# A two-layer graph kernel: eight of 26 adjacency chunks taken as products instead of six, sums in nine pairs, and the copy of a finished head on VectorE

## The reference

```python
q = (x @ Wq.T).reshape(d, n, h)      # k, v alike; d = 128, n = 3327, h = 8
a = jnp.einsum('dnh,dmh->dnm', q, k) * scale
a = a + spatial_encoding + edge_encoding          # both are adj
a = jax.nn.softmax(a, axis=2)
out = jnp.einsum('dnm,dmh->dnh', a, v)
```

## Time and profile before

| | us |
|---|---|
| median of 3 runs | 11010.36 |
| range of the runs | 11007.11 to 11011.85 |
| the profiled execution, its own time | 11014.46 |
| its span in the profile | 11012.8 |

### The profile page before, as it was taken

One profiled execution on the slowest core, in us unless ns is written; L12 is line 12 of the kernel. 1 busy time (PEld: TensorE's weight loads), 2 busy tenths in 40 slices (PEclk: granted clock), 3 DMA queues, 4 the chain that ended last, 5 costly groups with the idle time before them and its releaser, 6 DMA issues. The chain is left out here.

```text
span 11012.8 us, 545250 instructions
## 1 busy us (share of the span) xinstructions
PE 10687.6 (97%) x216535; PEld 6688.6 (61%) x216535; DVE 10342.3 (94%) x10893; ACT 10389.9 (94%) x9224; POOL 6451.1 (59%) x3236
## 2 busy tenths in 40 slices
PE   8749999999999999999999999999999999999998
PEld 6616666666666666666666666666665666666666
DVE  7679999999999999999999999999999999999997
ACT  3359999999999999999999999999999999999996
POOL 4345666666665666666665666666665666666664
PEclk9889999999999999999999999999999999999999
DMA  6581111111112111111112111111112111111113
GB/s 220 171 263 55 41 41 41 41 42 42 41 42 79 41 41 41 41 41 41 42 42 81 41 41 41 41 41 41 41 41 81 41 41 41 41 41 41 41 41 83
DMA packets 572794, 649.12 MB, mean 59 GB/s; under 512 B 172173, under 2 KB 511251, under 8 KB 566867
## 3 DMA queue, kind: packets, MB, share of 16 engines
q1 hardware_dynamic: 570130, 617.66, 20.1%
q0 software_dynamic: 832, 1.71, 0.0%
HBM read 485.17 MB, written 133.77 MB: 56 GB/s over the span
## 5 line engine op out<-in xcount | busy, mean ns | idle before, releaser
L1075 DVE SCALAR_TENSOR_TENSOR at_double<-attention_adj_t,at_score 128x832 f32<-128x832 f32 x10240 | 9672.9, 1014 | 411.0 <-PE at_score L1019 396.2
L999 POOL TENSOR_TENSOR at_single<-at_single,attention_adj_t 128x832 f32<-128x832 f32 x3072 | 6114.8, 1991 | 3977.4 <-ACT at_single L1089 3944.0
L1092 ACT ACTIVATE at_double<-at_double 128x1664 f32<-128x1664 f32 x5120 | 8138.8, 1653 | 28.1 <-DVE at_double L1075 20.8
L1019 PE MATMUL at_score<-at_q,at_k 128*32 128x512 bf16 (+1 forms) x106496 | 7275.9, 350 | 72.5 <-DMA at_v<-v_scratch 46.3
L1035 PE MATMUL at_acc<-at_double,at_v 128*9 128x208 f32 x81920 | 5387.0, 339 | 0.7 <-ACT at_double L1092 0.6
L1019 PEld LDWEIGHTS at_score<-at_q,at_k 128*32 128x32 bf16 x106496 | 3529.9, 145 | 2586.1 <-DVE at_double L1075 1145.3
L1089 ACT ACTIVATE at_single<-at_score 128x832 f32<-128x832 f32 x3072 | 2828.4, 921 | 34.2 <-PE at_score L1019 34.2
L1035 PEld LDWEIGHTS at_acc<-at_double,at_v 128*9 128x9 f32 x81920 | 2080.6, 91 | 1002.3 <-issue 3.8
L1035 PE MATMUL at_acc<-at_single,at_v 128*9 128x208 f32 x24576 | 1615.4, 339 | 2.9 <-issue 2.8
L1035 PEld LDWEIGHTS at_acc<-at_single,at_v 128*9 128x9 f32 x24576 | 622.8, 91 | 307.3 <-issue 4.8
L287 POOL TENSOR_TENSOR layer_col_acc<-layer_col_acc,st_a_rows 128x3328 f32<-128x3328 f32 x26 | 189.2, 7277 | 181.3 <-DMA st_a_rows<-in_adj_dram 181.3
(11 more groups left out here) (123 smaller groups left out, 1288.1 us busy)
## 6 DMA issues: line engine op xcount, KB each, us to landing
at_k<-k_parts_scratch SPq DMA_DIRECT2D x1536, 156.0 KB
at_q<-q_parts_scratch SPq DMA_DIRECT2D x4608, 13.0 KB
at_v<-v_scratch SPq DMA_DIRECT2D x512, 112.5 KB
adj_t_scratch<-st_a_t SPq DMA_DIRECT2D x26, 1664.0 KB, 7.6
st_a_rows<-in_adj_dram SPq DMA_DIRECT2D x25, 1663.5 KB, 8.7
attention_adj_t<-adj_t_scratch SPq DMA_DIRECT2D x16, 2080.0 KB, 16.7
attended_scratch<-at_o SPq DMA_DIRECT2D x1920, 7.3 KB
q_parts_scratch<-pr_partsq SPq DMA_DIRECT2D x39, 512.0 KB, 4.6
```

Source lines behind the costliest of these rows:

```text
L999: pool.tensor_tensor(slot(n), slot(n), at[:, plan.chunk[n], :], ALU.mult).then_inc(multiplied, 1)
L1019: last = pe.matmul(score[plan.buffer(n)][32 * t:32 * (t + 1), a:b], keys[:, 32 * t:32 * (t + 1)], q[k][:, a:b], start=True, stop=True, til ...
L1075: dve.scalar_tensor_tensor(out=slot(n), in0=at[:, plan.chunk[n], :], scalar=2.0, in1=score[plan.buffer(n)][:, 0:NB], op0=ALU.mult, op1=ALU ...
L1092: act.activation(doubles[buffer][:], doubles[buffer][:], ACT.Exp).then_inc(exped, 1)
```

## The change

PRODUCTS goes from 6 to 8: eight chunks of the 26 are taken as products, 18 as sums in nine pairs. DOUBLES goes from 8 to 6 and SINGLES from 4 to 8 (20 buffers of 128 x 832 in both). `Steps` then gives each head the order `ssPssPssPssPssPssPssPssPss`, and ScalarE's order is P, pair, P, pair; two pairs follow each other without a P between only at a head's end (steps 21-22 and 24-25; then the P of the next head's step 2, then its pair 0-1). `stream_adjacency` stores eight chunks as exp(2a); its chunks 18 and 19 need an activation of 128 x 256 of their own. The groups at a change of block become sums 0-4 and 5-9, products 18-22 (steps 2 to 14), sums 10-14 (steps 15 to 21), products 23-25 (steps 17, 20, 23) and sums 15-17 (steps 22, 24, 25).

The copy of a finished head moves from ScalarE (KEEP_LAG) to VectorE, behind step 12 of the next head (KEEP_AFTER). The counts of `kept` and `stored` are shifted by one, since the first copy copies an empty `acc`. ScalarE's loop is then a plain loop over all 128 bodies. SCORE_LEAD goes from 8 to 9. The number of instructions in TensorE's loop body is as before.

```diff
--- before.py
+++ after.py
@@ -46,11 +46,11 @@
 COLT = 4
 QW = NB // COLT
 assert QW * COLT == NB
-DOUBLES = 8
-SINGLES = 4
+DOUBLES = 6
+SINGLES = 8
 GROUP = 4
 CHUNKS_AT_ONCE = 5
-PRODUCTS = 6
+PRODUCTS = 8
 LIMIT = 30.0
 
 
@@ -912,8 +912,8 @@
         LOADS = 16 * (PARTS + PARTS * PARTS + 1 + 3)
         STORES = 16 * COLT
         CLEARED = 8
-        SCORE_LEAD = 8
-        KEEP_LAG = 5
+        SCORE_LEAD = 9
+        KEEP_AFTER = 12
         assert GROUP * products % SINGLES == 0 and GROUP % 2 == 0
 
         first_of_group = {steps[0]: g for g, steps in enumerate(plan.groups)}
@@ -956,7 +956,7 @@
 
             with runs(sp):
                 for k in range(2):
-                    sp.sem_inc(stored[k], STORES)
+                    sp.sem_inc(stored[k], 2 * STORES)
                 sp.wait_ge(prefetched, 16 * len(Steps(PRODUCTS).prefetched))
                 if products:
                     for g in plan.prefetched:
@@ -981,7 +981,7 @@
                                 load_adjacency(b + 1, range(len(plan.groups)))
                         store(b, HEADS - 2 + k, k)
                 for k in range(2):
-                    sp.wait_ge(stored[k], STORES * (BLOCKS * HEADS // 2 + 1))
+                    sp.wait_ge(stored[k], STORES * (BLOCKS * HEADS // 2 + 2))
 
         @block.gpsimd
         def _(pool):
@@ -1064,6 +1064,14 @@
                 dve.wait_ge(k_zero, 2)
                 for k in range(2):
                     dve.memset(k_all[k][SHIFT_ROW:SHIFT_ROW + PARTS, 0:N], 1.0).then_inc(cleared, 1)
+
+                def keep_head(i, b, head):
+                    k = head % 2
+                    dve.wait_ge(used, STEPS * i + (b * BODIES * STEPS + (head + 1) * C + AHEAD))
+                    dve.wait_ge(stored[k], STORES * (GROUP // 2) * i + STORES * (b * BODIES * (GROUP // 2) + head // 2 + 2))
+                    dve.tensor_copy(o[k][:], acc[k][:, 0:QW]).then_inc(kept, 1)
+
+                dve.sem_inc(kept, 1)
                 for b in range(BLOCKS):
                     with dve.Fori(0, BODIES) as i:
                         for n in range(STEPS):
@@ -1074,6 +1082,9 @@
                                 dve.wait_ge(used, plan.used_by(i, plan.last_like(plan.slot, n)) + (b * BODIES * STEPS + AHEAD))
                                 dve.scalar_tensor_tensor(out=slot(n), in0=at[:, plan.chunk[n], :], scalar=2.0,
                                                          in1=score[plan.buffer(n)][:, 0:NB], op0=ALU.mult, op1=ALU.add).then_inc(added, 1)
+                            if n % C == KEEP_AFTER:
+                                keep_head(i, b, n // C - 1)
+                keep_head(0, BLOCKS, -1)
 
         @block.scalar
         def _(act):
@@ -1091,26 +1102,10 @@
                     act.wait_ge(added, plan.of_kind_before(i, steps[-1] + 1, False))
                     act.activation(doubles[buffer][:], doubles[buffer][:], ACT.Exp).then_inc(exped, 1)
 
-            def keep_head(i, head):
-                act.wait_ge(used, STEPS * i + ((head + 1) * C + AHEAD))
-                act.wait_ge(stored[head % 2], STORES * (GROUP // 2) * i + STORES * (head // 2 + 1))
-                act.activation(o[head % 2][:], acc[head % 2][:, 0:QW], ACT.Copy).then_inc(kept, 1)
-
-            def body(i, more):
-
-                for m in range(KEEP_LAG, UNITS + KEEP_LAG):
-                    if m < UNITS or more:
+            with runs(act):
+                with act.Fori(0, BLOCKS * BODIES) as i:
+                    for m in range(UNITS):
                         exponential(i, m)
-                    if m % (UNITS // GROUP) == KEEP_LAG - 1:
-                        keep_head(i, m // (UNITS // GROUP) - 1)
-
-            with runs(act):
-                act.sem_inc(kept, 2)
-                for m in range(KEEP_LAG):
-                    exponential(0, m)
-                with act.Fori(0, BLOCKS * BODIES - 1) as i:
-                    body(i, True)
-                body(BLOCKS * BODIES - 1, False)
 
 
 def project_out(nc, o_d, out, keep):
```

## The result

The changed kernel took 11058.02 us (median of 5 runs, 11054.93 to 11062.00), the kernel before 11010.36 in the same comparison. The ratio is 1.0044, with a 95% interval of 1.0033 to 1.0055: 48 us slower. Forecast were 10862 us, in a range of 10838 to 10920.

A forecast was written before the change was run, and what follows sets the result against it. ScalarE was taken as the bound, at 19.49 us of a 19.60 us head. -109 (work) - 38 (gap) - 3 (block changes) + 2 (first stage) = -148 us from 11014.46 gave 10866, 10862 as median; range 10838 to 10920.

The forecast's parts named there:

- The step on ScalarE's work: Per head on ScalarE: one double fewer, two singles more, no copy; 19.28 us, 0.21 less, 109 us over 512 heads.
- ScalarE is the bound: ScalarE sets the pace before the change: 19.49 us of work in a head's period of 19.60 us.
- The copy leaves ScalarE: Taking the 0.22 us copy off ScalarE is what pays: -109 us; exchanging sums for products gains nothing there.
- The gap behind the wrap: ScalarE's 0.30 us wait per four-head body, at steps 6-7 behind the body's wrap, goes: -38 us.
- rival B: VectorE's copy or the one product buffer makes ScalarE wait 0.1 to 0.2 us a head: 10913 to 10964; 10%.
- VectorE's copy: On VectorE between steps 12 and 13: 0.37 us (0.19 to 1.01), making a head 17.5 us of 19.3.
- The cover: The product of step 14 still hides VectorE's copy, whose triple is 0.04 us late and made good in the next.
- TensorE: Scores of products share one buffer: that chain takes 1.7 us, under a triple's 2.225, and costs nothing.
- GpSimd, SyncE, the first stage: GpSimd's eight products, 15.3 us a head, cost 0; SyncE's issues hidden; first stage +2 us (0 to +14).
- Rival C: Back edge of TensorE's loop no longer hidden, 127 times: ScalarE loses 1.5 us a body, 11053 us; 5%.
- What would show it: Trace signs if right: 4096 and 4608 instructions, 0.744 and 1.481 us apart; VectorE idle 1.8 us a head; GpSimd about 82%.
- The mark for a wrong prediction: A head's period of 19.5 us or more, or ScalarE waiting on line 1089 for TensorE in most triples.

The follow-up runs named there:

- e1: The change with one exponential of a 128 x 1 tile ahead of ScalarE's loop: 10882.7 us, ratio 0.9883 to the kernel before.
- e9: The kernel before with ScalarE's loop made plain and one exponential of a 128 x 1 tile ahead of it: 11011.6 us, ratio 0.9998.
- e4: The kernel before with ScalarE's loop made plain over all 128 bodies, copy still on ScalarE: 11163.5 us, ratio 1.0137.
- e6: The change with a square root of a 128 x 1 tile ending each ScalarE pass, so two table loads a pass: 11335.3 us, ratio 1.0295.
- e7: No version of the kernel: only stretches of ScalarE's doubles, singles and copies, alone or beside GpSimd and VectorE; 292.9 us, one run.
- e3: The kernel before with eight products, 6 double and 8 single buffers, all else as before: 11000.7 us, ratio 0.9990.
- e5: e1 with SCORE_LEAD 8 in place of 9: 10883.8 us, ratio 0.9884 to the kernel before.
- e10: e1 without VectorE's copy, the result leaving out the attention: 10890.3 us, ratio 0.9887 to the kernel before.
- e2: e1 with six products, 8 double and 4 single buffers: 11121.5 us, ratio 1.0101 to the kernel before.
- e8: e1 with ten products, 4 double and 10 single buffers: 11823.7 us, ratio 1.0738 to the kernel before.

## Why the prediction was wrong

The direction failed on one missing term. The step on ScalarE's work says that a head "loses one double (-1.481), gains two singles (+1.488) and loses the copy (-0.22)", and stops there: the change's third edit there, the plain loop in place of a rotated and peeled one, has no sentence in the prediction. It was taken to be a matter of writing. In the kernel before the one load stands at 802.3 us, ahead of the peeled exponentials; without these nothing ahead of the loop asks for the table, and a load stands inside it, one for each pass. 128 x 1.37 us = 175 us turned a gain of some 128 into a loss of 48. That the loads go when one exponential stands ahead of the loop is shown (e1 against the change, e9 against e4); that the compiler places them by whether the table is known at the loop's head is inferred from that.

The trace of before held the warning. Line 335 is the first activation in the streaming loop, which has no such activation directly ahead of it, and its row shows 13 loads, one for each of the loop's 13 passes:

```profile
L335 ACT ACT_TABLE_LOAD  x13: 1283/1283/1283, 47.7 to 403.6; - x13
```

I had the count of these loads in view and did not connect it with a loop that was about to lose its prologue. The Trainium skill, "ScalarE: Activation LUTs", section "What ACT_TABLE_LOAD costs", gives 1283 ns for a load, and the trace agrees to the nanosecond. It adds a drain of some 1380 ns, which makes 2.66 us for every switch to a different set. The runs show less: where the same function runs before and behind the load, 1.52 us (e4) and 1.59 us (the change) were lost on the spot, and in e6, where two loads in a row change from exponential to square root and back, the next instruction starts 1.30 and 1.29 us behind the start of each load.

By the prediction's own steps:

- *ScalarE is the bound*: right. One instruction taken from its loop moved the time by 175 us.
- *The copy leaves ScalarE, -109 us*: right as to the distances from start to start (e7: 1.480 and 0.743, copies 0.223). The heads without the load have the forecast 19.31 us on average.
- *The gap behind the wrap, -38*: the gap went (e3, no head stands out), but in its place each head of e1 and e5 waits 0.07 us at its end, 0.07 x 512 = 36 us. That is rival B, in small. e1's gain of 128 us stands against the forecast's 148. Rival B's reason for so little, three engines within 8% of each other, was worked out slightly wrong: 17.5 is 9% under 19.28.
- *VectorE's copy*: 0.284 us from start to start in the trace after, 0.37 were taken; its record is 0.37. The cover was judged rightly with 18 sums (e10) and the bound with 20 would not have been (e2).
- *TensorE*: its chain through the one product buffer was put at nothing ("It costs nothing while 0.5 us of spare holds"). The rows of e1 show this chain ahead of the second double of a head's end, with the 0.07 us. The sum had 0.93 us for the exponential, whose record is 1.06 us long there; and it was made for a triple with a product in it, not for the two pairs in a row at a head's end.
- *GpSimd, SyncE, the first stage*: as forecast, within what can be told. The first single exponential started at 822.3 us instead of 821.2, with a table load of 1.28 us just ahead of it (in e1, 821.9), where +2 was taken for the first stage.
- *Rival C* named 11053 us, and 11058 came out, by another mechanism: it put a stall on TensorE's back edge, and what cost the time was a table load at the head of ScalarE's loop. TensorE's waits for issue did grow, from 9.2 to 65.8 us, but they are 52.8 in e1 and 23.8 in e5, and the two take the same time: nothing hangs on them. The near hit is luck and proves nothing.
- *What would show it*: the counts and the distances held, VectorE waits 1057.4 / 512 = 2.1 us a head for scores where 1.8 were named, and GpSimd is busy in 81% where 82% were named. The mark for a wrong prediction, a period of 19.5 us or more, is met: 78.80 / 4 = 19.70. The list had no entry for an instruction that should not be there.

The best version is e1 (and e5, the same within noise): the change with one exponential of a 128 x 1 tile ahead of the loop, 1.2% faster than before and 1.6% faster than the change.

## What to carry to other kernels

When an edit changes the form of a loop on the engine that bounds, read the engine's instruction kinds per pass before and after, and not only the work: here a prologue that looked like scheduling went, and a table load came into the loop. If a load turns up in each pass though the function never changes, run one tiny activation of the same function ahead of the loop. When work is shared out anew over a few buffers, look for neighbours in the order that need the same buffer (e8). And where an engine is the bound at 99%, look at which of its rows make up the busy time: here a table load hid in a busy share. A pause on one engine can also cost more than its length, when it stops TensorE and the granted clock falls (e6): read the clock of the short stretch behind the pause.

## What the runs showed of the hardware beyond that

Distances and lengths of ScalarE's records do not tell the same. In e7, 24 single exponentials from PSUM start 0.743 us apart throughout, but their records grow from 0.86 to 1.15 us, some 13 ns each; where singles and doubles alternate the doubles' records grow too (1.58 to 1.67), in a stretch of doubles alone they stay at 1.57 to 1.58, and at the start of the next stretch, behind a pause, a single's record is 0.86 again. In e1 the records of singles are 1.06 us long at a head's end and 0.98 at its start. What waits for such an exponential, here a score's buffer, waits for the record's end and not for the next start: the load of 4547.43 stands 0.05 us behind the record's end at 4547.38, while the next double had started at 4547.06. My bound for the chain through the product buffer had used 0.93.
